# Projections inside attention as 24 half-height matmuls, with a new order of the eight steps of a unit

## The reference

```
q, k, v = (proj(w_q), proj(w_k), proj(w_v))            # of layernorm(x), heads of 16
attn = softmax(einsum('bhqd,bhkd->bhqk', q, k) / sqrt(16))
x = x + einsum('bse,oe->bso', (attn @ v), w_o)
w_eff = clip(round(w / (mean(abs(w)) + 1e-5)), -1, 1) * mean(abs(w)) * s   # for gate, up, down
x = x + bitlinear(int8_quant(up * relu(gate)**2), w_down)
```

## Time and profile before

| | us |
|---|---|
| median of 3 runs | 991.39 (988.03 to 992.25) |
| the profiled execution | 990.27, its span 988.5 |
| PE busy | 928.7 (94%) |
| DVE busy | 834.2 (84%) |
| ACT busy | 759.2 (77%) |

### The profile page before, as it was taken

The page is one execution under the profiler, slowest core; times in us unless marked ns, Lnnn a source line. Parts: engine busy times, 40 slices in busy tenths (PEclk is TensorE's granted clock), DMA queues, the critical chain, the costliest instruction groups (busy, mean ns, idle before and its releaser), DMA issues.

```text
span 988.5 us, 16486 instructions
## 1 busy us (share of the span) xinstructions
PE 928.7 (94%) x5790; PEld 286.9 (29%) x5806; DVE 834.2 (84%) x1516; ACT 759.2 (77%) x1408; POOL 157.5 (16%) x298
## 2 busy tenths in 40 slices
PE   4799999999999999999999999999889988899997
PEld 3343222222222222222222222222122224444443
DVE  6597999999999999999999999999883237878873
ACT  4322689888888888988999899988886657866664
POOL 3500012111121111212211123111112210112100
PEclk9899999999999999999999999999999999999998
DMA  8310111131021123312232112513340004411000
GB/s 298 94 37 1 33 38 39 34 78 41 23 55 50 48 55 95 96 34 60 76 121 54 38 39 82 121 54 103 114 137 12 12 10 131 137 43 43 33 22 33
DMA packets 38041, 64.90 MB, mean 66 GB/s; under 512 B 3654, under 2 KB 19014, under 8 KB 37702
## 3 DMA queue, kind: packets, MB, share of 16 engines
q1 hardware_dynamic: 37958, 63.85, 22.3%
HBM read 42.27 MB, written 21.23 MB: 64 GB/s over the span
## 4 chain that ended last, share of the span: by engine, by line
PE 71%; ACT 15%; DVE 6%; issue 5%; DMA 2%; SPq 1%; POOL 0%; ACTq 0%; POOLq 0%; DVEq 0%
PE ps L446 21%; PE ps L429 12%; PE ps L385 12%; PE ps L363 8%; ACT PB L773 6%; PE ps L590 6%; PE ps L326 4%; DVE mx L1014 3%; PE ps L638 3%; PE ps L614 3%; ACT PB L857 1%; ACT XV L835 1%; PE ps L412 1%; DVE XV L1108 1%; DMA tu<-wkT 1%
## 5 line engine op out<-in xcount | busy, mean ns | idle before, releaser
L1014 DVE TENSOR_REDUCE mx<-ps 128x1 f32<-128x512 f32 x1024 | 635.4, 683 | 49.8 <-PE ps L385 43.5
L773 ACT ACTIVATE PB<-ps 128x512 f32<-128x512 f32 x1024 | 537.2, 600 | 93.8 <-PE ps L429 93.1
L429 PE MATMUL ps<-QK 50*128 50x512 f16 x1024 | 301.0, 384 | 15.2 <-ACT PB L773 13.9
L385 PE MATMUL ps<-QK 48*128 48x512 f16 x1024 | 303.1, 385 | 10.2 <-issue 5.6
L446 PE MATMUL ps<-PB,Vg 128*32 128x512 f32 x2048 | 274.6, 608 | 1.6 <-ACT PB L773 0.8
L385 PEld LDWEIGHTS ps<-QK 48*128 48x128 f16 x1024 | 75.5, 93 | 206.5 <-DVE mx L1014 175.5
L429 PEld LDWEIGHTS ps<-QK 50*128 50x128 f16 x1024 | 73.0, 93 | 197.1 <-ACT PB L773 148.7
L363 PE MATMUL ps<-XV,wqk 128*128 128x512 f16 x384 | 111.4, 386 | 1.1 <-DVE wmean L951 1.1
L1247 POOL TENSOR_SCALAR nmb<-nm 128x16 f16<-128x16 f32 x32 | 6.6, 206 | 539.1 <-DVE nm L1019 539.1
L590 PE MATMUL ps<-wo,XV 128*128 128x512 f32 x128 | 61.0, 609 | 0.0
L446 PEld LDWEIGHTS ps<-PB,Vg 128*32 128x32 f32 x2048 | 40.4, 108 | 69.9 <-issue 47.7
(11 more groups left out here) (126 smaller groups left out, 654.1 us busy)
## 6 DMA issues: line engine op xcount, KB each, us to landing
parts_d<-spl SPq DMA_DIRECT2D x64, 128.0 KB
att_d<-OS SPq DMA_DIRECT2D x32, 256.0 KB
QK<-parts_d SPq DMA_DIRECT2D x48, 128.0 KB, 4.5
QK<-parts_d SPq DMA_DIRECT2D x16, 256.0 KB, 4.2
XV<-att_d SPq DMA_DIRECT2D x2, 2048.0 KB, 8.6
QK<-rden_d SPq DMA_DIRECT2D x8, 512.0 KB, 7.5
wqk<-x SPq DMA_DIRECT2D x16, 256.0 KB, 3.9
out<-PB SPq DMA_DIRECT2D x16, 256.0 KB, 2.0
```

What stands on the lines that cost most here:

```text
L385: nc.tensor.matmul(ps[:, at % S_BANKS, :], QK[rows, sup % 2, 2 * set_ + p, 0, half * HALF + qt * P:half * HALF + (qt + 1) * P], QK[rows, s ...
L429: nc.tensor.matmul(ps[:, tile_bank_of(place), :], QK[rows, sup % 2, 2 * set_ + p, 1, kt * P:(kt + 1) * P], QK[rows, sup % 2, 2 * set_ + p, ...
L773: nc.scalar.activation(PB[:, at % 3, i, :], ps[:, tile_bank_of(tile_place(sup * 4 + step // KEYT, step % KEYT, i)), :], ACT.Exp, scale=exp ...
L1014: nc.vector.tensor_reduce(mx[:, v % 2, idx, kh:kh + 1], ps[:, at % S_BANKS, :], AX.X, ALU.max).then_inc(s_used, 1)
```

## The change

```diff
-MEAN_BANK = 7
+MEAN_COLUMN = 256
+ORDER = ("STtsTAhthshs", "htthsThsAsTshR", "hshthsTsTASth", "hsThtSTsASt",
+         "TtShShhhTShStA", "StShThhtSsTA", "tTTssSAthS", "tSThTShStAs")
+SCORE_SIDES = tuple("Ss".index(c) for c in "".join(ORDER) if c in "Ss")
+TILE_SIDES = tuple(tuple("Tt".index(c) for c in step if c in "Tt") for step in ORDER)
+PIECES_BEFORE = tuple("".join(ORDER[:r]).count("h") for r in range(9))
+HALF_PIECES = 24
...
-            return k // 8, k // 4 % 2, 1 - k % 2, k // 2 % 2
+            side = SCORE_SIDES[k]
+            c = SCORE_SIDES[:k].count(side)
+            return c // 4, c // 2 % 2, side, c % 2
+
+        def tile_head(r, i):
+
+            side = TILE_SIDES[r][i]
+            return 2 * TILE_SIDES[r][:i].count(side) + side
...
+        def mean_at(w):
+
+            return ps[:, rows_bank(WEIGHT_MEANS[w] + 1), MEAN_COLUMN + w:MEAN_COLUMN + w + 1]
+
         def pe_mean(pe, w):
 
             pe.wait_ge(w_tot, w + 1)
-            pe.wait_ge(job_copy, WEIGHT_MEANS[w] + JOBS_AHEAD)
-            nc.tensor.matmul(ps[:, MEAN_BANK, 8 * w:8 * w + 1], ones[:], wtot[:, w:w + 1], start=True, stop=True)\
+            pe_tile_free(pe, rows_place(WEIGHT_MEANS[w] + 1))
+            nc.tensor.matmul(mean_at(w), ones[:], wtot[:, w:w + 1], start=True, stop=True)\
                 .then_inc(w_psum, 1)
...
+        def pe_job_free(pe, n):
+
+            pe.wait_ge(job_copy, n)
+            pe.wait_ge(w_low, 5)
+            if n == JOBS_AHEAD:
+                pe.wait_ge(rows_used, 1)
...
-                    if n - JOBS_AHEAD in WEIGHT_MEANS:
-                        pe.wait_ge(w_step, 3 * WEIGHT_MEANS.index(n - JOBS_AHEAD) + 1)
+                    pe_job_free(pe, n)
...
+        def pe_half_job(pe, n, m):
+
+            sup, qk, half = job_of(n)
+            side, c = m // (3 * KT), m % (3 * KT)
+            k, (a, b) = c // 3, PRODUCTS[c % 3]
+            if m == 0:
+                pe_job_free(pe, n)
+            if m == 3 * KT:
+                pe.wait_ge(job_top, n - JOBS_AHEAD + 1)
+            group, rows = sup % SPB, slice(side * SIDE, side * SIDE + SIDE)
+            last = nc.tensor.matmul(ps[:, job_bank(n), :], wqk[rows, qk, a, k, group * P:(group + 1) * P],
+                                    xparts[sup // SPB][rows, b, k, half * HALF:(half + 1) * HALF],
+                                    start=(m == 0), stop=(m == HALF_PIECES - 1))
+            if m == 3 * KT - 1:
+                last.then_inc(job_top, 1)
+            if m == HALF_PIECES - 1:
                 last.then_inc(job_psum, 1)
 
...
+                if at in WEIGHT_MEANS:
+                    pe.wait_ge(w_step, 3 * WEIGHT_MEANS.index(at) + 1)
...
-            side, p = i % 2, i // 2
+            p, side = tile_head(kt, i) // 2, tile_head(kt, i) % 2
...
-                elif r == 4:
-                    tile(0)
-                    score(0)
-                    pieces(4, 7)
-                    score(1)
-                    tile(1)
-                    score(2)
-                    tile(2)
-                    score(3)
-                    tile(3)
-                    values()
-                elif r == 5:
...
+                scores, tiles, halves = 0, 0, PIECES_BEFORE[r]
+                for what in ORDER[r]:
+                    if what in "Ss":
+                        score(scores)
+                        scores += 1
+                    elif what in "Tt":
+                        tile(tiles)
+                        tiles += 1
+                    elif what == "h":
+                        piece(halves)
+                        halves += 1
+                    elif what == "A":
+                        values()
+                    else:
+                        means()
+                        rows()
...
+                if r == 1 and at > 0:
+                    act_sums(act, at - 1)
                 act_exp(act, sup, step, 0)
                 act_exp(act, sup, step, 1)
                 act_exp(act, sup, step, 2)
-                if r == 0 and at > 0:
-                    act_sums(act, at - 1)
...
-            nc.vector.tensor_scalar(wmean[:, w:w + 1], ps[:, MEAN_BANK, 8 * w:8 * w + 1], 1.0 / (INTER * HID), None, ALU.mult)\
+            dve.wait_ge(rows_used, WEIGHT_MEANS[w] + 2)
+            nc.vector.tensor_scalar(wmean[:, w:w + 1], mean_at(w), 1.0 / (INTER * HID), None, ALU.mult)\
...
-                    if r == 1:
+                    if r == 2:
                         dve_factor(dve, WEIGHT_MEANS.index(at))
```

More of the change, by code:

```diff
@@ L212, in build @@
         job_psum, job_copy, job_split, spl_step = sem("job_psum"), sem("job_copy"), sem("job_split"), sem("spl_step")
+        job_top = sem("job_top")
         parts_out = [sem(f"parts_out{r}") for r in range(2)]
@@ L366, in pe_job @@
             if m == 3 * KT - 1:
+                last.then_inc(job_psum, 1)
+        def pe_half_job(pe, n, m):
[13 more added lines that the diff above has]
+            if m == HALF_PIECES - 1:
                 last.then_inc(job_psum, 1)
@@ L465, in values, with piece @@
                         pe_av(pe, (at * KEYT + r - LATE) // STEPS, (at * KEYT + r - LATE) % STEPS)
-                def pieces(first, end):
+                def piece(m):
                     if job_in(at):
-                        for m in range(first, end):
-                            pe_job(pe, job_in(at), m)
+                        pe_half_job(pe, job_in(at), m)
                 def rows():
@@ L478, in means @@
                         pe_mean(pe, WEIGHT_MEANS.index(at))
-                if r == 0:
-                    tile(0)
-                    tile(1)
-                    score(0)
-                    tile(2)
-                    score(1)
-                    score(2)
-                    values()
-                    score(3)
-                    tile(3)
[L490 to L524, removed]
-                elif r == 4:
-                    tile(0)
-                    score(0)
-                    pieces(4, 7)
[L529 to L535, removed]
-                elif r == 5:
[L537 to L567, removed]
@@ L772, in act_exp @@
                 act.wait_ge(av_done, at - 2)
-            nc.scalar.activation(PB[:, at % 3, i, :], ps[:, tile_bank_of(tile_place(sup * 4 + step // KEYT, step % KEYT, i)), :],
+            nc.scalar.activation(PB[:, at % 3, tile_head(step % KEYT, i), :], ps[:, tile_bank_of(tile_place(sup * 4 + step // KEYT, step % KEYT, i)), :],
                                  ACT.Exp, scale=exp_reg).then_inc(probs, 1)
```

## The result

The changed kernel takes 1003.82 us (median of 4 executions, 1001.01 to 1006.15) and the one before, run beside it, 991.74 (988.03 to 992.25): a ratio of 1.0125, 95% interval 1.0089 to 1.0161. It is slower, by 12.1 us where 6.6 were forecast. The profiled execution took 1006.15, the longest of the four, at a mean granted clock of 0.985 (the shortest had 0.990); so its span is read piece by piece before it is set against the medians.

What follows compares the result with a forecast made beforehand. The prediction took PE (20.0 us of work a unit) and DVE (19.4), nearly level with three banks between, as the bound. 1.6 + 3.5 + 1.5 + 1.5 = 8.1 us on 990.3 gave 998, range 987 to 1005.

Steps and rivals of the forecast that it cites:

- The plain unit: Units without absolute values, signs or mean: saved height changes offset by lone slots and waits; +0.1 us in each of 16.
- h starts within 0.01 of S or T of the other side: Sign on PE that half pieces overlap with scores or transposes; a start 0.2 later would mean no overlap.
- the thirteenth piece starts 0.44 behind the twelfth: First piece of side 1 on PE must wait for the last of side 0: 0.22 us more a unit.
- the fifth S of step 4: On PE, this score needs the second's bank, starting at 1.77 instead of 1.54: 0.23 us lost.
- matmuls start in order: PE: two of one side in a row leave the other half empty; 47 slots against 44, 0.65 us more a unit.
- the layout: Unit laid out by hand from trace distances; gave 20.4 and 22.0 for the old order, beside 20.44 and 22.03 measured.
- PE and DVE are nearly level: In a plain unit PE works 20.0 us and DVE could do 19.4, with only three banks between them.
- Rival (b): Faster: PE's own work decides and the S banks suffice; 26 x 0.40 = 10 us less, 980; chance 0.16.
- Units with absolute values or signs: T waits behind ACT's long instructions, later h and S meet lone slots: 0.35 us more in each of ten, 3.5.
- Behind the jobs: Units 26 to 31, only S, T and A: 0.7 us each in units 27 and 28, 1.5 in all.
- The mean: Where the mean is added, DVE waits for ACT's row copy and R comes later: 0.5 us for each of three, 1.5.
- The sums: ACT's sums moved behind the fourth exponential: cost nothing, as A of step 1 comes late; uncovered they would cost 0.48.

Runs made afterwards that it cites:

- the fifth experiment: Changed kernel, but the opening's 64 scores of units 0 and 1 take their sides in turn as before; 998.89 us, ratio 1.0096 to the kernel before.
- the fourth experiment: Kernel before, old order and full pieces, with only the sums and the mean at their new places; 1000.97 us, ratio 1.0096.

## Why the prediction was right, and where it was not

The direction and the range held (998 forecast, 987 to 1005, measured 1003.8). The mechanism held for the plain unit: the changes of height that half pieces save are given back, and the period stays. The size was half of what came. That the time still lies in the range owes something to luck: of the 15.9 us between the two profiled executions, 10.8 are parts that the sum did not have.

**The plain unit.** Forecast 20.5 to 20.6, measured 20.46, just below. (There are fourteen plain periods before 399.59 us, not thirteen.) Four finer readings came as the prediction has them: h starts within 0.01 of S or T of the other side; the thirteenth piece starts 0.44 behind the twelfth; DVE's idle time is 0.6 in a window, 0.4 before; the fifth S of step 4 waits 0.22, forecast 0.23. Timeline of PE in the changed kernel, then its step 4, and DVE's group in the window from 219.08:

```profile
221.43 0.38 PE L399 MATMUL ps<-XV,wqk 64*128 64x512 f16 x1
221.44 0.38 PE L423 MATMUL ps<-QK 48*128 48x512 f16 x1
221.65 0.37 PE L399 MATMUL ps<-XV,wqk 64*128 64x512 f16 x1
221.87 0.38 PE L469 MATMUL ps<-QK 50*128 50x512 f16 x1
222.09 0.39 PE L399 MATMUL ps<-XV,wqk 64*128 64x512 f16 x1
...
225.17 0.82 PE L423 MATMUL ps<-QK 48*128 48x512 f16 x2
...
225.60 0.09 PEld L423 LDWEIGHTS ps<-QK 48*128 48x128 f16 x1 [0.50 <-DVE mx L981]
```

```profile
L981 DVE TENSOR_REDUCE mx<-ps 128x1 f32<-128x512 f32 x33 | 20.5, 683 | 0.6 <-PE ps L423 0.3
```

At 221.65 and 222.09 stand the twelfth and the thirteenth piece. No gap stands between a half piece and an S. With that, the trace agrees with the Trainium skill, TensorEngine Tiling, section Key Properties, by which only a change of the tiling mode drains the engine.

The step "matmuls start in order" failed in its detail. The S at 221.44 stands behind the h of 221.65 in the program, and by its recorded start it ran ahead of it, beside the h before: its half was free and its bank too. No slot was saved by it: the h of 221.65 now stands alone, since the next matmul starts at 221.87. The Trainium skill, TensorE: Matmul & The Clock Gate, Part 3, says that matmuls start and end in program order; the recorded starts here speak against the first half of that. Why the period came out 0.1 shorter than the layout had it stays open.

**What bounds the unit.** "PE and DVE are nearly level" holds, and more strictly than I used it. I let DVE's 19.4 and PE's 20.0 stand as floors that could be reached. Ten pieces less gave 0.21, reductions over three quarters of the columns 0.41. Rival (b), in which PE's own work decides and 10 us come back, is refuted by the few pieces. That 20.05 is left when DVE needs 15.99 and ACT 18.13 of it suggests that PE's own order, with A's block and its waits for exponentials, is the next limit right behind. That is argued, not shown: with short reductions the loads of S still wait 4.8 us in the unit for DVE (6.2 with whole ones), and no run separates these waits.

**Units with absolute values or signs.** 0.35 forecast, 0.33 measured, ten times: 3.3 for 3.5. The size was right. The reason given for it, the lone slots of steps 5 to 7, is not tested; the runs with cut instructions show only that the 0.33 hangs on ACT's whole ones. The term missed what hangs on such a unit. The step that failed is in "Behind the jobs": the clock was counted for units 27 and 28 alone ("if it adds one, 1.7 are lost"), though units 15 to 26 have the same long waits of T, and in the profiled execution four of them lost 1.55 each. That is the largest part missing, 6.2 us of this execution. In the medians it is less, since the falls come in some executions and not in others: the four ran at 0.985, 0.989, 0.985 and 0.990, those at the lower clocks 4.5 us above the others. That falls cost time is shown by the same work at 23.91 and 22.36; why they come in those units of this kernel and not in the same units of the fifth experiment is open.

**The opening.** "The six jobs of the opening stay as they were": true, but its scores did not. That step was an omission: the function that gives a score its side is used there too. 3.4 us, shown by the fifth experiment.

**The mean.** 0.5 forecast for each of three, 1.5; measured about nothing. The two with a job cost 0.68 where they cost 0.90 (0.38 in the unit and 0.30 in the next). The forecast added 0.2 for the lateness of ACT's copy and 0.2 for R; how much of either came was not looked at. The third, without a job, costs 0.5 more, its 0.37 and 0.12 in two periods. **Behind the jobs**: 1.5 forecast, 1.5 measured, with falls at 720.6 and 737.7 in place of 699.4 and 723.3. The parts did not come as forecast, 0.7 in each of units 27 and 28. Windows of unit 27 in the changed kernel and, with the old order and no fall, in the fourth experiment:

```profile
696.49:720.03 23.54, 20.36 (x133) 5.21 (x133) 21.14 (x35) 20.19 (x37) 4.70 (x8) 1.00 0.47 154
```

```profile
698.55:720.77 22.22, 19.50 (x133) 4.82 (x133) 20.59 (x34) 20.00 (x38) 4.28 (x7) 1.00 0.49 161
```

Before, unit 27 took the same 23.54 with a fall in it. So without falls the new order costs 1.32 there, not 0.7. Both falls of the changed kernel lie in the period of unit 28, 25.35 long. At 1.55 a fall 22.25 is left, against 23.71 - 1.32 = 22.39 before, so by this estimate the order costs nothing in unit 28.

**The sums.** "They cost nothing" failed as a general step: 0.29 in one order, 0.43 with the opposite sign in the other. In the new order the place chosen was the right one, so the sum did not suffer.

By terms, against the profiled spans: forecast 1.6 + 3.5 + 1.5 + 1.5 = 8.1; the same terms measured 0.3 + 3.3 + 0.0 + 1.5 = 5.1. Opening 3.4, falls 6.2 and the end's 1.2 were not in the sum at all.

## What to carry to other kernels

When engines are level within 2% (here PE 20.42 and DVE 19.99 of 20.44), take work from each in an experiment before crediting a saving on one: here 2 us of PE's work bought 0.2, and 3.9 of DVE's 0.4. Look for the longest single stop, not only for the busiest engine: cutting ACT's long instructions in two and spreading the halves gave 1.4%, where the reordering of PE gave nothing. And where a table takes over an index rule, list every caller of that rule, above all those outside the loop that the table was written for.

## What the runs showed of the hardware

- A matmul on a free half of the array started 0.21 us ahead of one that precedes it in the program and whose half was busy (221.44 and 221.65), by the recorded starts.
- Less work can be slower through the clock: with 4 of 24 pieces the changed kernel had a mean clock of 0.976 and took 1008.83 us, with all of them 1003.82. A fall lasts 3.4 us at half clock in the trace and costs such a unit 1.55. The three kernels with less work had four (kernel before, few pieces), nine (changed, few pieces) and six (short reductions) such falls in units 14 to 26 of their profiled executions; the kernel before had none, the changed one four and that of the fifth experiment none.
- Executions of one kernel spread with the clock: the kernel with short reductions took 983.59 to 984.02 us at 0.992 to 0.993, and 992.12 to 994.98 at 0.981 to 0.982. A comparison of medians carries some us of that.
- Half-height pieces over 64 rows overlap with an S or T of the other half: the starts are within 0.01 us (221.43 and 221.44). Beside S and T a plain unit with them takes 20.47, with full pieces in the same places 23.41; in blocks they cost 1.25 over full pieces.
